# A group's token rows fetched as 32x32 blocks and transposed by VectorE; up weights copied once into one DRAM block per expert

## What is computed

```python
h = h + _L0_ffn_ref(_layernorm(h))
# in _L0_ffn_ref, xt are the 2304 normalised rows:
route_prob = softmax(xt @ Ws + bs); p = max(route_prob); routes = argmax(route_prob)
h = gelu(einsum('td,edf->tef', xt, W1) + b1)      # 192 -> 768, per expert
out = einsum('tef,efd->ted', h, W2) + b2          # 768 -> 192, per expert
final = where(routes == 0, common * p/p, p * out[routes] + (1 - p) * out[0])
```

## Time and profile before

| | |
|---|---|
| profiled execution, its time | 386.88 us |
| its span (first to last instruction) | 385.0 us |
| granted TensorE clock, mean | 0.993 |
| PE busy | 364.3 us (95%) |
| PE weight loads busy | 325.6 us (85%) |
| POOL / DVE / ACT busy | 188.3 / 172.2 / 163.9 us |
| DMA packets, bytes | 40589, 49.58 MB |

### The profile page before, as it was taken

One profiled execution on the slowest core, in us unless ns is written; L12 is line 12 of the kernel. 1 busy time (PEld: TensorE's weight loads), 2 busy tenths in 40 slices (PEclk: granted clock), 3 DMA queues, 4 the chain that ended last, 5 costly groups with the idle time before them and its releaser, 6 DMA issues. The chain is left out here.

```text
span 385.0 us, 10445 instructions
## 1 busy us (share of the span) xinstructions
PE 364.3 (95%) x3291; PEld 325.6 (85%) x3292; DVE 172.2 (45%) x595; ACT 163.9 (43%) x553; POOL 188.3 (49%) x307
## 2 busy tenths in 40 slices
PE   6799999999999999899999999998999999999991
PEld 5677877788888888788888899997999999999991
DVE  3365767777777787544232265411112211111111
ACT  0122233333333354778444454335545544555540
POOL 1657977777777787443013006740333333444333
PEclk9999999999999999999999999999999999999997
DMA  7764335353321435435000905626666776676630
GB/s 243 234 207 120 101 105 162 94 156 91 90 79 48 130 113 166 124 97 187 20 0 14 245 2 142 217 80 147 150 170 160 176 187 164 167 165 164 155 76 0
DMA packets 40589, 49.58 MB, mean 129 GB/s; under 512 B 10412, under 2 KB 32313, under 8 KB 40553
## 3 DMA queue, kind: packets, MB, share of 16 engines
q1 hardware_dynamic: 34641, 42.95, 37.8%
q0 software_dynamic: 5024, 5.72, 8.8%
q10 hardware_dynamic: 888, 0.45, 0.4%
HBM read 39.84 MB, written 10.27 MB: 130 GB/s over the span
## 5 line engine op out<-in xcount | busy, mean ns | idle before, releaser
L641 PE MATMUL bank<-W,ARENA 128*128 (+1 forms) x516 | 94.6, 334 | 1.5 <-issue 1.2
L641 PEld LDWEIGHTS bank<-W,ARENA 128*128 128x128 f32 x516 | 82.8, 190 | 5.7 <-issue 1.5
L1371 POOL DMA_INDIRECT out<-ARENA,ID x25 | 39.4, 1575 | 71.3 <-DVE ARENA L1236 62.0
L855 ACT ACTIVATE ARENA<-score_banks,B1R 128x128 f32<-128x128 f32 x150 | 41.5, 376 | 39.8 <-PE score_banks L631 24.1
L855 ACT ACTIVATE ARENA<-score_banks,B1T 128x128 f32<-128x128 f32 x108 | 29.9, 375 | 31.8 <-PE score_banks L631 31.8
L1269 POOL TENSOR_TENSOR VS<-V,R 108x384 f32<-108x384 f32 x32 | 27.7, 865 | 30.5 <-DVE R L960 30.2
L1232 DVE TENSOR_TENSOR ARENA<-bank,B 128x192 f32<-128x192 f32 x25 | 8.9, 358 | 71.6 <-PE bank L641 71.6
L623 PE MATMUL score_banks<-RINGS,W1R 128*128 128x128 f32 x300 | 37.8, 276 | 1.4 <-ACT RINGS L795 0.8
L623 PEld LDWEIGHTS score_banks<-RINGS,W1R 128*128 128x128 f32 x300 | 35.6, 192 | 1.8 <-issue 1.8
L1260 POOL TENSOR_TENSOR RINGS<-QK,GM 128x216 f32<-128x216 f32 x64 | 34.1, 553 | 3.4 <-PE score_banks L579 3.4
L579 PEld LDWEIGHTS score_banks<-QK,RINGS 48*108 48x108 f32 x512 | 28.7, 171 | 6.1 <-issue 2.9
(11 more groups left out here) (149 smaller groups left out, 622.1 us busy)
## 6 DMA issues: line engine op xcount, KB each, us to landing
W1R<-in_w SPq DMA_DIRECT2D x25, 384.0 KB
V<-v_rows SPq DMA_DIRECT2D x96, 54.0 KB
W<-in_w SPq DMA_DIRECT2D x9, 576.0 KB, 4.2
W1R<-in_w_rest SPq DMA_DIRECT2D x50, 96.0 KB
ARENA<-in_patches SPq DMA_DIRECT2D x11, 384.0 KB, 3.6
packed_tokens<-RINGS POOLq DMA_DIRECT2D x1, 2425.0 KB, 13.2
ARENA<-packed_tokens SPq DMA_DIRECT2D x25, 97.0 KB, 2.8
PT<-in_patches SPq DMA_DIRECT2D x6, 384.0 KB, 3.2
```

What stands on the lines that cost most here:

```text
L641: last = pe.matmul(bank[2 * par][:, 0:D], HT[par][:, c * P:c * P + P], W2[:, bass.ds((expert * FC + c) * D, D)], start=c == 0, stop=c == F ...
L855: last = act.activation(HT[par][:, to:to + P], bank[6 + g][:, c * P:c * P + P], ACT.Gelu, bias=b1[:, bias:bias + 1])
L1371: pool.indirect_dma_start(out, bass.IndirectOffsetOnAxis(ap=ID[par][:, 0:1], axis=0), YR[par], None, bounds_check=TOKENS - 1, oob_is_err=F ...
```

## The change

Two things are changed, both in how a group's operands arrive.

Rows: `load_blocks` reads the 192 features of a group in six DMAs of 32 features each. Each writes 32 partitions: partition b gets, of rows b, 32+b, 64+b and 96+b, the 32 features side by side, so that each 32x32 square of `XF` is a square of the rows at the place of its transpose. DVE's `transpose` (32x32 squares) then gives `XTF` in three instructions (128x128, and 64x128 twice). PE's transposes and ACT's copies of the groups are gone, and with them `ffn_t_done`.

Weights: in main steps 11, 13, ... 25 SP issues three DMAs each from DRAM to DRAM, which put one expert's up weights into `w1_blocks` in the layout of `W1R`. A group's up weights then come with one DMA of 128 rows of 4608 bytes.

```diff
+BLOCK_UP_START = MIXER_START + 1
+    w1_blocks = nc.dram_tensor("w1_blocks", (EXPERTS * P, WCOLS), F32, kind="Internal").ap()
-        XF = [cut(ROW) for _ in range(2)]
+        XF = [cut(2 * P) for _ in range(2)]
             def load_group_up(n, par):
                 expert = sp.value_load(GROUP_EXPERT[0:1, bass.ds(n, 1)], min_val=0, max_val=EXPERTS - 1)
-                load_up(W1R[par], expert, w1_in[par])
+                sp.dma_start(W1R[par][:, :], w1_blocks[bass.ds(expert * P, P)]).then_inc(w1_in[par], 16)
+            def block_up(e):
+                sp.dma_start(w1_blocks[e * P:e * P + P, 0:DFF], w1[:, e * DFF:(e + 1) * DFF]).then_inc(w1_blocked, 16)
+                for g in range(2):
+                    at = e * P + g * DB
+                    sp.dma_start(w1_blocks[at:at + DB, DFF:WCOLS],
+                                 w1_rest[0:DB, e * DFF + g * FH:e * DFF + (g + 1) * FH]).then_inc(w1_blocked, 16)
+            def load_blocks(n, par):
+                rows = packed[bass.ds(n * P, P)] if not isinstance(n, int) else packed[n * P:n * P + P]
+                for f in range(D // BLOCK):
+                    row, at = f % (P // BLOCK) * BLOCK, f // (P // BLOCK) * P
+                    sp.dma_start(XF[par][row:row + BLOCK, at:at + P].rearrange("b (j a) -> b j a", a=BLOCK),
+                                 rows[:, f * BLOCK:(f + 1) * BLOCK].rearrange("(j b) a -> b j a", b=BLOCK)).then_inc(xr_in[par], 16)
+                if BLOCK_UP_START <= s < BLOCK_UP_START + 2 * (EXPERTS - 1) and (s - BLOCK_UP_START) % 2 == 0:
+                    block_up((s - BLOCK_UP_START) // 2 + 1)
             sp.wait_ge(groups_ready, 1)
+            sp.wait_ge(w1_blocked, 16 * 3 * (EXPERTS - 1))
             for r in range(2):
-                sp.dma_start(XF[r], packed[r * P:r * P + P]).then_inc(xr_in[r], 16)
+                load_blocks(r, r)
             def load_group(i, ks):
                 n, par, half = tile_at(i, ks[0])
-                sp.wait_ge(ffn_t_done, n - 1)
-                sp.dma_start(XF[par], packed[bass.ds(n * P, P)]).then_inc(xr_in[par], 16)
+                sp.wait_ge(ffn_xt, n - 1)
+                load_blocks(n, par)
-            def transpose_group(i, k):                                    # PE
-                ...
-                transpose_tile(XF[par], bank[4 + par]).then_inc(ffn_t_done, 1)
-            two_by_two(pe, group_step, (0, 1, 2), GROUPS)
+            two_by_two(pe, group_step, (1, 2), GROUPS, start=1)
-            def copy_group(n, par):                                       # ACT
-                act.wait_ge(ffn_t_done, n + 1)
-                copy_twice(XTF[par], bank[4 + par]).then_inc(ffn_xt, 1)
# DVE, main_step, ahead of add_common(ky):
+                if s == MAIN_END - 1:
+                    for n in range(2):
+                        transpose_group(n, n, 0, False)
+            def transpose_group(n, par, half, guard):
+                dve.wait_ge(xr_in[par], 16 * (D // BLOCK) * (half + 1))
+                if guard:
+                    dve.wait_ge(f1_done, 2 * (TILES + n - 1))
+                dve.transpose(XTF[par][:, 0:P], XF[par][:, 0:P])
+                for g in range(2):
+                    last = dve.transpose(XTF[par][g * DB:g * DB + DB, P:2 * P], XF[par][0:DB, P:2 * P])
+                last.then_inc(ffn_xt, 1)
# DVE, group_step:
+                    transpose_group(n, par, half, True)
                     copy_b1(n, par, True)
```

More of the change, by code:

```diff
@@ L50 @@
 EPS = 1e-5
+BLOCK = 32
 GROUPS = (TOKENS + (EXPERTS - 1) * (P - 1)) // P
@@ L236, in vit_kernel @@
         expert_w_in = sem("expert_w_in")
+        w1_blocked = sem("w1_blocked")
         patch_in = [sem(f"patch_in{i}") for i in range(3)]
@@ L283, in vit_kernel @@
         xn2_ready = sem("xn2_ready")
-        ffn_t_done = sem("ffn_t_done")
         ffn_xt = sem("ffn_xt")
@@ L668, in route @@
                           start=False, stop=True).then_inc(router_done, 1)
-            def transpose_group(i, k):
[L671 to L674, removed]
-                transpose_tile(XF[par], bank[4 + par]).then_inc(ffn_t_done, 1)
             def transpose_xn2(t):
@@ L751, in _ @@
                       (TILES,) * 4 + (PAIR_STEPS,) * 2 + (TILES,) * 5)
-            for n in range(2):
-                transpose_group(0, n)
             def group_step(i, ks):
-                kt, kf, kh = ks
-                if kt is not None and kt >= 2:
-                    transpose_group(i, kt)
+                kf, kh = ks
                 if kf is not None:
                     n, par, half = tile_at(i, kf)
-                    pe.wait_ge(w1_in[par], 48 * (half + 1))
+                    pe.wait_ge(w1_in[par], 16 * (half + 1))
                     pe.wait_ge(ffn_xt, n + 1)
@@ L889, in _ @@
                       (TILES,) * 3 + (PAIR_STEPS,) * 2 + (TILES,) * 3)
-            def copy_group(n, par):
-                act.wait_ge(ffn_t_done, n + 1)
-                copy_twice(XTF[par], bank[4 + par]).then_inc(ffn_xt, 1)
             def group_step(i, ks):
[L896 to L908, removed]
+                kg, = ks
+                n, par, half = tile_at(i, kg)
+                act.wait_ge(b1_copied, n + 1)
+                gelu(TILES + n, par, B1R[par], True)
+            two_by_two(act, group_step, (0,), GROUPS)
         @block.vector
```

## The result

The changed kernel takes 400.09 us (median of 4 runs, 398.34 to 401.65) where the kernel before took 388.56 (4 runs, 387.5 to 389.47): a ratio of 1.032 (95%: 1.028 to 1.036). Slower, as forecast, by three quarters of the amount.

A forecast was written before the change was run, and what follows sets the result against it. PE was taken as the bound before, SP's issues as the loop's bound after. 386.9 + 8.1 + 9.2 - 1.5 = 402.7 us profiled, 403.8 median, 4% slower; own range 398 to 411, 394 to 414 for 8 in 10.

The forecast's parts named there:

- start, weights of group 2 issued: Start of the groups: ten more DMAs ahead of the store delay these weights from 265.21 to 273.3, +8.1 us.
- loop, 22 periods: Group loop: SP becomes the bound, a period of 4.95 us instead of 4.53, +9.2 us in all.
- end, last weights to up projection 24: End of the loop: PE waits for the weights' landing, 4.2 us after issue instead of 5.7, -1.5 us.
- copies of the weights: Main steps: 24 more SP issues by 0.45 us fit where SP mostly waits; zero, without the cover up to 10.8.
- The lower clock: Start: after 7.9 us idle PE restarts at 1.2 GHz; up projection 0 takes about 3.9 us instead of 2.3.
- (d): SP's loop chain: six row DMAs per group at 0.56 to 0.62 us each, 3.4 to 3.7 in all.
- The low bound of the same row: SP's loop: shortest DMA instruction, 0.29 us, gives 4.3 a group; PE then binds at 4.35, -4.0 us.
- PE's idle time: Group loop: PE idle some 0.6 us a group, the weights' DMA as releaser, clock 1.00.
- rival 3: Group loop: 128-byte pieces make the DMA engines the bound, 5.5 us a group, 415.9 us total; chance 0.06.
- rival 1: Group loop: PE stays the bound at 4.35 us if an issue costs 0.29; 389.2 us total; chance 0.07.
- rival 2: Start: SP's issues don't delay the store, so the kernel gains; 385.5 us at 0.05 an issue; chance 0.04.
- rival 4: Main steps 18 to 25: copies make V rows late, up to 10.8 us more, 412 to 415; chance 0.05.

## Why the prediction was right, and where its size was off

The time went the forecast way; the sum was 15.8 us and the measured difference of the two profiled executions 11.5 (398.34 - 386.88). By terms:

| term | forecast | measured | from |
|---|---|---|---|
| start, weights of group 2 issued | +8.1 | +8.5 | 273.67 against 265.21 |
| loop, 22 periods | +9.2 | +4.6 | 4.74 against 4.53 |
| end, last weights to up projection 24 | -1.5 | -1.6 | 4.09 (382.14 - 378.05) against 5.7 |
| copies of the weights | 0 | 0 | the experiment with them alone |

- **The start, step by step.** The twelve issues took 5.56 us (forecast 5.6), `base` of tile 16 came at 267.00 (267.15) behind the store, up projection 0 at 268.40 (268.6), its end at 272.88 (272.5), and the weights at 273.67 (273.3). The lower clock cost it more than forecast: 4.5 us instead of 3.9. Moving the store confirms the cause. The lower clock was forecast for one up projection; the second ran with 12 issues in 2.90 us, too, from 273.99.
- **The loop: the mis-sized term.** That SP becomes the bound, and by its count of issues, is shown twice (a DMA of SP's moved to ACT: 4.36; two more on SP: 5.92). The step that failed is the price in (d), 0.56 to 0.62 for each row DMA: six took 2.83 to 2.87 us, 0.50 from one to the next, because the DMA instruction took 0.317 us (median of 150) and not 0.37 to 0.43. I had taken the price from trains of static DMAs, and for those it was right: the twelve static ones at the start of the groups ran at 0.47 each. In the loop, where each stands behind a register operation and a move (0.19 with the gaps, as forecast), the instruction itself is shorter. The low bound of the same row (0.29) lay nearer to the truth than the median. With the right price (d) is 6 x (0.317 + 0.19) = 3.0 us and the forecast's sum 4.45; the measured 4.64 is longer because the other terms were set too low, by 0.2 together (0.97 from the last row issue to the weights' for 0.90, 0.36 for 0.34, the loop's branch 0.27 for 0.17). So two errors of opposite sign met, and the larger one, the row issue, gave the sum its direction. The 0.10 between 4.64 and 4.74 are 2.2 us in 22 periods: one wait on an up projection (0.5 us) and two trains with a long issue (3.55 us from 279.21 and 3.88 from 294.54, for 2.87).
- **The end.** The size is right, the reason only in part. The weights of the last group landed about when up projection 24 began (3.8 us after the issue, in the median), but no wait is listed there: it follows PE's down projection (380.08, 2.22 us) without a gap. PE's last wait for weights is the one before (0.27 us, up projection 23).
- **PE's idle time**, forecast as 0.6 a group, was 0.4 by the periods (4.74 - 4.35), and the view by stretches shows only 2.1 us of it in 60. Up projections behind a wait are drawn longer (1.60 us instead of 1.50); it seems that a PE that is starved a little looks busy. The wait for the weights' DMA is listed for 8 groups only.
- **The DMA engines** (rival 3) fall: a share of 0.68 in the loop as before, with 57023 packets instead of 40589; and with the issues moved to ACT the loop ran at PE's pace with a share of 0.72. The rule of the Trainium skill that spoke for it ("DMA: Bandwidth & Descriptors", Specifications, under 512 bytes no line rate) shows no cost in the time here: 128 pieces of 128 bytes landed 2.1 us after their issue, in the median. Some load there is: share times period gives 3.4 us of each DMA engine per group with the weights as before (0.57 x 5.92), where it was 3.1 (0.68 x 4.57); that is an estimate, and within the forecast's 0.4 to 1.3 less the present rows' 0.3.
- **PE stays the bound** (rival 1) and **faster** (rival 2) fall for the changed kernel, but what they say is what the kernel is once SP is relieved: with ACT's queue and the stores first the loop's gain is there (from up projection 2 to 24 it took 95.8 us instead of 100.4; 22 x 0.22 = 4.8 was forecast), and the start takes back a part of it: 0.7% of 388.6, 2.7 us, are left.
- **The copies** (rival 4) fall: from 0 to 200 us PE was busy for 190.8 us (189.6 before), the row train began at 257.69 (257.73), and the version with the copies alone ran at 1.001. Their issues were dearer than my 0.45 (0.52 and 0.60 us), without any effect, because SP had the room.

## What to carry to other kernels

When a change splits a DMA or adds some, write down the issuing engine's whole list for one period and price it like any other engine's work, address arithmetic included: PE's 4.35 us and SP's 4.74 are the whole story of this loop, and no table of busy time shows SP. Such work moves to another engine's queue if that engine has room; here that, together with stores moved out from behind the twelve new issues, turned 3% slower into 0.7% faster. Look at what stands behind the issues that you add, in the first round above all: a wait that PE's own work did not have (a transpose moved to an engine with another queue of waits) costs more there than in the loop.

## What the runs showed of the hardware

- The DMA instruction on SP took 0.317 us in the register-addressed loop and 0.43 in a static train (twelve in 5.56 us), with equal shapes (32 partitions of 4 times 32 elements). I had not expected it to depend on that, and can't say why it does. The Trainium skill says of issuing from several engines that it saves only the sequencer's time, "which is usually small relative to the DMA itself" ("DMA: Bandwidth & Descriptors", Issuing engines are not separate DMA queues); here these 0.3 to 0.5 us, seven times a group, were the bound.
- The issue price does not grow with the pieces (0.43 us for 3200 of them), but the issues behind such a DMA do: two stores in 3.39 us instead of 0.91, six row DMAs in 4.02 instead of 2.72 (one of them took 1.64, the median is 0.43). It was there before, hidden: four stores in 3.24.
- A DMA from DRAM to DRAM costs SP 0.52 to 0.60 us to issue.
- VectorE transposes 128x128 float32 in 32x32 squares in 0.31 us and 64x128 in 0.28, so half the partitions save a tenth.
- The clock's fall after an idle time of about 2 us is not regular: it came with 1.87 and 2.08 us and stayed away with 1.91, the last in a single execution, of 391.12 us. After waits of 3.2, 4.0 and 7.7 us the clock was down each time.
